# A fused transformer block and expert mixture on one core: kept sums, inverses and spreads per tile, and moves in three engines' lists

## What is computed

```python
# layer 0
h = ln(x) * (1 + sc_msa) + sh_msa
x = x + self_attn(h) * g_msa                 # 16 heads, windows of 128, rolled by 64
h = ln(x) * (1 + sc_mca) + sh_mca
q, (k, v) = h @ w_q + b_q, context @ w_kv + b_kv          # 77 context tokens
scores = q k^T / 4
top_s, top_i = top_k(scores, 16)             # of 77, for each head and token
o = softmax(top_s) @ v[top_i]
x = x + (o @ w_co + b_co) * g_mca
x = x + swiglu(ln(x) * (1 + sc_mlp) + sh_mlp) * g_mlp     # hidden 1024
# layer 1
nx = layer_norm(x) * gamma + beta
weights = softmax((nx @ Wq) (prototypes @ Wk)^T / 16)     # 77 prototypes
evidence = weights @ (prototypes @ Wv)
combined = [nx, evidence, anchor]
router_probs = softmax(combined @ router_W + router_b)    # 3 experts
h = silu(combined @ e_w1 + e_b1);  routed = sum_e router_probs_e * (h_e @ e_w2 + e_b2)
g = sigmoid(silu(combined @ gate_w1 + gate_b1) @ gate_w2 + gate_b2)
out = x + g * (routed @ out_w + out_b)
```

## Time and profile before

| | us |
|---|---|
| median of 3 runs | 1443.78 (1443.26 to 1445.39) |
| the profiled execution | 1448.53 |
| its span, first to last instruction | 1446.7 |
| PE busy | 1404.7 (97%) |
| DVE busy | 1066.6 (74%) |
| ACT busy | 818.8 (57%) |
| POOL busy | 440.5 (30%) |

### The profile page before, as it was taken

The page is one execution under the profiler, slowest core; times in us unless marked ns, Lnnn a source line. Parts: engine busy times, 40 slices in busy tenths (PEclk is TensorE's granted clock), DMA queues, the critical chain, the costliest instruction groups (busy, mean ns, idle before and its releaser), DMA issues.

```text
span 1446.7 us, 29891 instructions
## 1 busy us (share of the span) xinstructions
PE 1404.7 (97%) x9585; PEld 1177.1 (81%) x9585; DVE 1066.6 (74%) x4754; ACT 818.8 (57%) x2523; POOL 440.5 (30%) x600
## 2 busy tenths in 40 slices
PE   6999999999999999999999999999999999998997
PEld 5778788888888788888888788888888878887886
DVE  3485868788796878879697777869688786968632
ACT  2473374747556384665747466574757547474433
POOL 1314132323315232331335132232334313232302
PEclk9999999999999999999999999999999999999999
DMA  7520000010010000010010000000010000000000
GB/s 244 178 93 2 1 2 25 2 34 9 19 33 13 4 2 25 1 34 1 23 36 1 16 1 16 11 20 16 9 35 17 16 2 7 3 1 9 1 2 14
DMA packets 32760, 35.29 MB, mean 24 GB/s; under 512 B 8744, under 2 KB 27868, under 8 KB 32349
## 3 DMA queue, kind: packets, MB, share of 16 engines
q1 hardware_dynamic: 32605, 33.38, 7.6%
HBM read 28.83 MB, written 4.22 MB: 23 GB/s over the span
## 4 chain that ended last, share of the span: by engine, by line
PE 73%; DVE 21%; issue 3%; ACT 1%; POOL 1%; SPq 0%; DMA 0%; DVEq 0%; POOLq 0%; ACTq 0%
PE bank L964 16%; PE bank L1033 11%; PE bank L973 8%; PE bank L1009 7%; DVE knocked L2266 7%; PE bank L824 6%; PE bank L1016 4%; PE bank L873 4%; DVE M L2259 3%; PE bank L810 2%; PE bank L863 2%; DVE M L2254 2%; PE bank L885 2%; PE bank L781 2%; PE bank L924 2%
## 5 line engine op out<-in xcount | busy, mean ns | idle before, releaser
L964 PE MATMUL bank<-hB,Wm 128*128 128x256 f32 x1024 | 244.0, 385 | 2.5 <-ACT hB L1404 2.5
L964 PEld LDWEIGHTS bank<-hB,Wm 128*128 128x128 f32 x1024 | 191.8, 191 | 34.2 <-issue 7.0
L1009 PE MATMUL bank<-nxT,W1nx 128*128 128x256 f32 x896 | 212.6, 383 | 0.0
L1443 ACT ACTIVATE prob<-bank,rmax 128x128 f32<-128x128 f32 x512 | 180.8, 433 | 29.6 <-DVE rmax L2193 29.6
L1801 POOL TENSOR_TENSOR scores<-scores,M 128x308 f32<-128x308 f32 x128 | 94.8, 741 | 315.3 <-DVE knocked L2266 313.1
L1033 PE MATMUL bank<-W2p,gT 128*128 128x256 f32 x768 | 183.2, 381 | 3.0 <-DVE acc L2345 1.9
L1009 PEld LDWEIGHTS bank<-nxT,W1nx 128*128 128x128 f32 x896 | 166.5, 191 | 23.3 <-issue 2.8
L1033 PEld LDWEIGHTS bank<-W2p,gT 128*128 128x128 f32 x768 | 141.2, 190 | 23.8 <-issue 2.8
L1493 ACT ACTIVATE tbs<-bank,b1half 128x256 f32<-128x256 f32 x128 | 60.8, 475 | 144.6 <-PE bank L964 140.6
L1509 ACT ACTIVATE tbs<-bank,betaH 128x256 f32<-128x256 f32 x224 | 96.1, 493 | 80.2 <-PE bank L1016 79.0
L1443 ACT ACTIVATION_READ_ACCUMULATOR prob<-bank,rmax 128x1 f32 x512 | 139.7, 273 | 0.0
(11 more groups left out here) (240 smaller groups left out, 2817.6 us busy)
## 6 DMA issues: line engine op xcount, KB each, us to landing
Wm_g<-in_L_xcond_w_m_dram SPq DMA_DIRECT2D x4, 1024.0 KB, 5.4
W1ev<-in_L_xcond_e_w_dram SPq DMA_DIRECT2D x6, 512.0 KB, 7.4
x<-in_x_dram SPq DMA_DIRECT2D x16, 128.0 KB, 2.7
x<-in_x_dram SPq DMA_DIRECT2D x32, 64.0 KB, 2.3
Wm<-in_L_xcond_w_m_dram SPq DMA_DIRECT2D x1, 2048.0 KB, 9.8
out_dram<-acc SPq DMA_DIRECT2D x16, 128.0 KB, 1.7
out_dram<-acc SPq DMA_DIRECT2D x32, 64.0 KB, 2.0
batch_rows<-row_store SPq DMA_DIRECT2D x4, 384.0 KB, 3.9
```

What stands on the lines that cost most here:

```text
L964: m = pe.matmul(bank_of(name)[:, half * UT:(half + 1) * UT], Wm1[:, k, c:c + P], hB[:, k, :], start=(k == 0), stop=(k == CB - 1))
L1009: pe.matmul(bank_of(name)[:, n * UT:(n + 1) * UT], W1nx[:, k, c0 + n * P:c0 + (n + 1) * P], nxT[:, k, :], start=(n == 0 and k == 0), stop= ...
L1443: m = act.activation(prob[:, s, i, :], psum[s][:, i * P:(i + 1) * P], ACT.Exp, bias=rmax[:, t, s * HPS + i:s * HPS + i + 1], accum_out=rsu ...
```

## The change

It does six things. The kept sums are inverted tile by tile (`a_invert_kept(t, u)`), and POOL spreads them tile by tile (`a_spread_kept(t, u)`), tile 0 ahead of the shift of kept tile 1. PE waits for each tile's spread by itself, and takes the tiles in the outer loop. In PE's list the router stands ahead of the turned kept inverses, and `a_v(1)` ahead of the picks y02 and y03. In ACT's list y03's copy stands ahead of the prototype's exponential, and each `a_kept_exp` directly behind a `a_cross_exp`, so that `a_kept_exp(1)` is now ahead of `b_tanh_first("h00")`. In DVE's list the bias of the queries, the pick (1, 0) and the sum and inverse of tile 0 stand ahead of parts of the last top-k blocks.

```diff
@@ -890,11 +890,14 @@
 
             def a_turn_inverses(name, values, u):
 
-                pe.wait_ge(spread if values == "pv" else spread_x, u + 1)
                 wait_free(pe, name, u)
                 bk = bank_of(name)
-                for f in range(CB):
-                    for t in range(1 if values == "pv" and u >= 2 else TILES):
+                if values == "pv":
+                    pe.wait_ge(spread, u + 1)
+                for t in range(1 if values == "pv" and u >= 2 else TILES):
+                    if values == "xv":
+                        pe.wait_ge(spread_x, u * TILES + (t + 1))
+                    for f in range(CB):
                         v = each[values][:, t, f * (H // CB):(f + 1) * (H // CB), :].rearrange("p h d -> p (h d)")
                         m = pe.transpose(bk[:, f * UT + t * P:f * UT + (t + 1) * P], v, ident[:, :])
                 m.then_inc(full[JOB[name][0]], 1)
...
@@ -1217,11 +1220,11 @@
                 a_q(a)
                 a_v(0, a)
                 b_turn_normed(b)
+                a_v(1, a)
                 a_turn_picked(0, 2, c)
                 if r == 1:
                     pe.wait_ge(readB, batch * 5 + 5)
                 a_turn_picked(0, 3, c)
-                a_v(1, a)
                 b_proto_scores(b)
                 b_first_nx("h00", 0, b)
                 b_first_nx("h01", 2 * P, b)
...
@@ -1239,8 +1242,8 @@
                 a_turn_picked(1, 2, c)
                 a_turn_picked(1, 3, c)
                 b_first_evidence("h10", RH, b)
+                b_router(b)
                 a_turn_inverses("r2", "xv", c)
-                b_router(b)
                 a_cross_values(1, c)
                 a_scores(0, range(SLOTS), a)
                 b_first_evidence("h11", RH + 2 * P, b)
...
@@ -1654,17 +1657,17 @@
                 a_keys(a)
                 b_affine(b)
                 a_copy_picked(0, 2, c)
+                a_copy_picked(0, 3, c)
                 b_proto_exp(b)
                 a_cross_exp(1, 0, c)
-                a_copy_picked(0, 3, c)
+                a_kept_exp(0, c)
                 a_copy_values(a)
                 b_copy_weights(b)
                 a_cross_exp(1, 1, c)
-                a_kept_exp(0, c)
                 if r == 1:
                     act.wait_ge(doneB, batch + 1)
+                a_kept_exp(1, c)
                 b_tanh_first("h00", hE[:, 0], 0, 0, b)
-                a_kept_exp(1, c)
                 a_copy_picked(1, 0, c)
                 a_copy_picked(1, 2, c)
                 a_copy_picked(1, 3, c)
...
@@ -1811,16 +1814,16 @@
 
             def a_spread(values, u):
 
-                if values == "pv":
-                    pool.wait_ge(sums_inverted, u + 1)
-                    inv = rinv
-                else:
-                    pool.wait_ge(kept_inverted, u + 1)
-                    inv = kinv
+                pool.wait_ge(sums_inverted, u + 1)
                 alone(pool)
-                for t in range(1 if values == "pv" and u >= 2 else TILES):
-                    i = pool.tensor_copy(each[values][:, t], inv[:, t, :].rearrange("p (h a) -> p h a", a=1).to_broadcast([P, H, D]))
-                i.then_inc(spread if values == "pv" else spread_x, 1)
+                for t in range(1 if u >= 2 else TILES):
+                    i = pool.tensor_copy(each[values][:, t], rinv[:, t, :].rearrange("p (h a) -> p h a", a=1).to_broadcast([P, H, D]))
+                i.then_inc(spread, 1)
+
+            def a_spread_kept(t, u):
+
+                pool.wait_ge(kept_inverted, u * TILES + (t + 1))
+                pool.tensor_copy(kept[:, t], kinv[:, t, :].rearrange("p (h a) -> p h a", a=1).to_broadcast([P, H, D])).then_inc(spread_x, 1)
 
             def gate(w, n, b, done):
 
...
@@ -1953,8 +1957,9 @@
                 a_shift(1, 1, c)
                 a_shift(1, 2, c)
                 a_shift(1, 3, c)
+                a_spread_kept(0, c)
                 a_shift_kept(1, c)
-                a_spread("xv", c)
+                a_spread_kept(1, c)
                 b_mix_biases(b)
                 if r == 0:
                     gate_b(batch)
...
@@ -2230,9 +2236,9 @@
                 by_slot = ksum[:, t, :].rearrange("p (f s e) -> p s f e", f=CB, e=PAR)
                 dve.tensor_reduce(by_slot, kept[:, t].rearrange("p (s f e) k -> p s f e k", f=CB, e=PAR), AX.X, ALU.add).then_inc(kept_sum, 1)
 
-            def a_invert_kept(u):
-                dve.wait_ge(kept_sum, u * TILES + TILES)
-                dve.reciprocal(kinv[:, :, :], ksum[:, :, :]).then_inc(kept_inverted, 1)
+            def a_invert_kept(t, u):
+                dve.wait_ge(kept_sum, u * TILES + (t + 1))
+                dve.reciprocal(kinv[:, t, :], ksum[:, t, :]).then_inc(kept_inverted, 1)
 
             def a_residual(dst, src, name, u):
                 dve.wait_ge(biased[("so", "co", "mo").index(name)], u + 1)
...
@@ -2535,15 +2542,16 @@
                 b_proto_shift(b)
                 a_topk("b", 1, 1, c)
                 b_proto_norm(b)
+                a_bias_queries(a)
                 a_topk("a", 1, 3, c)
+                a_pick(1, 0, c)
                 a_topk("b", 1, 2, c)
+                a_sum_kept(0, c)
+                a_invert_kept(0, c)
                 a_topk("b", 1, 3, c)
-                a_pick(1, 0, c)
-                a_bias_queries(a)
                 a_pick(1, 1, c)
-                a_sum_kept(0, c)
                 a_sum_kept(1, c)
-                a_invert_kept(c)
+                a_invert_kept(1, c)
                 b_silu("h00", hE[:, 0], 0, b)
                 b_route_shift(b)
                 a_normalise("xv", oT2, c)
```

More of the change, by code:

```diff
@@ L1923, in prologue @@
                 a_spread("pv", 1)
-                a_spread("xv", 0)
+                a_spread_kept(0, 0)
+                a_spread_kept(1, 0)
                 rstd_of(1, EPS0, 1)
@@ L2465, in prologue @@
                 a_sum_kept(1, 0)
-                a_invert_kept(0)
+                a_invert_kept(1, 0)
                 a_normalise("pv", oT, 1)
```

3 lines of the change are left out of this document (2 added, 1 removed).

## The result

| | before | after |
|---|---|---|
| median (us) | 1444.59 | 1493.3 (1492.36 to 1494.05, 4 runs) |
| the profiled execution (us) | 1448.53 | 1493.76 |
| its span (us), mean granted clock | 1446.7, 0.990 | 1491.9, 0.969 |

The ratio after over before is 1.0333, with a 95% interval from 1.0318 to 1.0348. The median before is of four executions, one of which took 2895.49 us; of the other three it is 1443.78, the value that the forecast started from. The forecast was 1474.6, 18.7 us less than measured, and its range ended at 1493.0, 0.3 us short of the result. The sign and the wait came out as predicted; the share of the clock was put at half of what it was. The mean granted clock is 0.969 in all four executions after, so the profiled one is no odd one.

A forecast was written before the change was run, and what follows sets the result against it. TensorE (PE) was taken to bound the kernel, so a loss would be a new PE wait. 16.8 us of later y12 plus 14.0 us of clock falls gave 30.8, on 1443.8: 1474.6 us, range 1457.8 to 1493.

The forecast's parts named there:

- What bounds the kernel: PE, busy 1404.7 of 1446.7 us; each step is DVE's row to pick(1,1), then PE's row from y12.
- The exponential ahead of h00: On ACT it delays h00's drain, so PE's y12 starts late: 1.2 us per step, 16.8 us in 14.
- Sums and inverses per tile: On DVE, the first sum and inverse put 0.61 us more ahead of pick(1,1), 0.2 more in all.
- Router moved, and the edits costed at nothing: PE's 0.61 us wait for inverses goes, 14 times, 8.5 us; moved bias, second values and y03's copy cost nothing.
- D: h00 done in time, DVE's 0.61 us more cancels PE's 0.61 less: no gain or loss, 1443.8; chance 0.04.
- E: PE's 0.61 us wait goes and y12 stays in place: 8.5 us faster, 1435.3; chance 0.04.
- The last step: Cross-only last step: h00 done at 1350.97, before y12 is due at 1351.45, so no cost.
- The clock: About 2.15 us of PE idleness before y12 halves the clock in 8 of 14 steps: 14.0 us lost.
- rival C: Clock falls in nearly every step, some longer than 3.4 us: 1485 to 1493; chance 0.12.
- The base: Forecast starts from the median of three runs, 1443.8 us; the profiled execution lies 4.7 us above it.

The follow-up runs named there:

- e5: The changed kernel with 9 unused identity products on PE filling the wait between y10 and y12 in the 14 steps; 1462.5 us.
- e1: The changed kernel with only the exponential of kept tile 1 put back behind h00's tanh group on ACT; 1450.12 us.
- e2: The kernel before with only the exponential of kept tile 1 moved ahead of h00's tanh group on ACT; 1444.17 us.
- e6: The changed kernel with DVE's order of bias, picks and sums, and POOL's shift ahead of the spread, as before; sums still per tile; 1436.37 us.
- e3: The changed kernel with DVE's order of bias, picks and sums as before, sums still per tile, POOL's order left as changed; 1539.39 us.
- e8: The changed kernel with only the bias of the queries put back behind the last top-k block on DVE; 1452.75 us.
- e7: As e6, with the bias of the queries behind the second pick on DVE, and y10 turned and copied after y12 and y13; 1444.16 us.

## Why the prediction was right in kind and too small

**What bounds the kernel.** Held. The wait for POOL went, and a wait before y12 took its place, released by h00's last instruction.

**The exponential ahead of h00.** Held to a tenth. With the shift of 2.69 us between the two profiles, the prediction's times are: last top-k block 260.70, POOL's shift 261.56, h00 drained 264.13, y12 264.19, cross values 266.64. The rows have 260.71, 261.53, 264.05, 264.19 and 266.67. The growth of a step without a fall was to be 1.2 us (14 x 1.2 = 16.8); it was 1.24 in the three such steps, and 17.5 over 14 in e5. e1 and e2 show that both halves are needed.

**Sums and inverses per tile.** Slightly off: DVE's pick(1,1) came 262.26 - 2.69 - 258.79 = 0.78 us later, not 0.61. The block itself came on time, so the 0.17 arose between its start and the pick. The rows place it. Pick(1,1) now stands directly behind the block whose last replacement it waits for, and starts 0.33 us after that replacement's start (261.93, 262.26). Before, pick(1,0) stood there, which needs nothing of this block, and started 0.14 after it (257.16, 257.30); in e6 it is 0.14 again, and in e1 0.34. In after it is hidden behind ACT's wait; in e1 it counts: 0.78 later on DVE less the 0.61 at the inverses is 0.17, measured 0.19 a step.

**Router moved, and the edits costed at nothing.** Held: the wait of 0.61 is gone, and e6 shows its worth undisturbed, 0.58 a step. One small thing was missed: PE now reaches the prototype's weights (L997) earlier than DVE has them (DVE's norm starts at 252.90 before and at 255.59 - 2.69 = 252.90 after), the 3.3 us of waits named above. The rivals D (no change) and E (8.5 us faster) were not wrong as places, but as states of this kernel: they need h00 drained in time, and that is what e1 and e6 establish. E gave 1435.3; e6 gave 1436.4.

**The last step.** Held: 14 waits, not 15, and all growth lies in the 14 steps.

**The clock: the term that was mis-sized.** I took 8 falls at 1.75 us, 14.0 us. There were 11, worth 27.9. Two factors. The number: I let the single row of 2.19 us of idleness stand for about half of the steps, and at 2.16 to 2.48 it was 11 of 14. The length, which weighs more: I took 3.4 us at half clock from the earlier trace rows for each, and 7 of the 11 lasted 6.8. A fall of 3.4 us cost 1.5 rather than 1.75. (The price of the row itself was sound: its 32 matmuls take 8.86 us with the fall, and 7.17 in e6, where none came, 1.69 less.) Eleven falls of 1.5 us would have been 16.5; the seven long ones add the rest, 1.6 us each. The prediction had this in rival C ("some lasting longer than 3.4 us, as the stretch of small matmuls behind the wait might"), whose end was the nearest to the time, but gave it 0.12. What spoke for it was in view: behind the wait of the earlier trace rows stood 32 matmuls of 128x256, and behind the new one stand transposes, 3-column products and 32-row products. That this is what made seven falls last longer is argued, not shown: the three kinds of step (0, 3.4, 6.8 us) have the same instructions behind the wait, and no run changed what stands there.

The Trainium skill (TensorE: Matmul & The Clock Gate, section "HAM oscillation — how this bites in real kernels"), which the prediction cites, describes waits of about 3 to 5 us, once in each iteration, with the clock down behind every one. The traces agree for waits of that length: it fell behind the wait of 3.54 us in the last cross step in all 12 kernels profiled, and in all 14 steps of e3 with 3.63 us or more. That is no forecast for the 2.2 us here, which are shorter, and behind which it fell in 11 of 14.

**The base.** The sum was 30.8 us; profile against profile it was 45.2. That is 14.4 us of the 18.7 missed, nearly all of it the clock (27.9 against 14.0). The other 4.3 are the base: before's profiled execution lay 4.7 us above the 1443.8 that the forecast started from, and after's only 0.5 above its median. The spread of before goes with the granted clock: the 14 executions beside e8 have a mean of 0.990 in those at 1448 us and of 0.992 in those at 1443 to 1444. Why it differs there stays open.

## What to carry to other kernels

Moving an instruction to the front of a list is safe only if what it waits for is also early, in the same version of the kernel: ask of each moved instruction what releases it there, and which engine waits for the one now behind it. Here one move was harmless without the other (0.2 us) and cost 42.8 us with it; the link between them, a bank that passes from h00 to y12, appeared in no wait of the profile of before. A gain can also hide a loss: DVE's order cost 10.9 us, and the 8.3 us won by the rest of the change left 2.6 of it to be seen. When an order is changed on one engine, walk the chain through every other list that feeds or follows it (e3: one POOL instruction left in its place cost 100 us against e6), and price a wait on TensorE of about 2 us with the clock as well as with its own length: the clock's share was here larger than the wait's.

## What the hardware showed that I had not expected

**Half clock costs more than the wait, and useless work is cheaper than idleness.** The wait before y12 lengthens the steps by 17.5 us, the falls behind it by 27.9. Nine products in each step that nothing reads made the kernel 31 us faster. Idleness at this place against falls, over all kernels:

| idle us at the place | falls |
|---|---|
| 0.15 to 0.5 (e5, after the filler), 0.5 to 0.6 (e7), 0.7 to 0.95 and 0.5 (e8), 1.1 to 1.3 (e1) | none in 14 steps each |
| 2.16 to 2.48 (after) | 11 of 14 |
| 3.63 to 3.70, in the last cross step 2.92 (e3) | 15 of 15 |

**The same wait falls or not.** Steps with the same instructions and 2.16 us (step 2, no fall) or 2.17 us (step 3, 6.8 us at 0.50) of idleness behave differently. The waits behind the 14 steps show the same. They are alike in all 12 kernels profiled: the clock fell behind the one of 3.54 or 3.55 us in 12 of 12, behind the one of 2.19 us (`hB`) in 7 of 12, and behind one of 1.03 us in 3 of 12 (after, e6 and e7). In e6 it was the longer one that passed, and the shorter one that was followed by 0.50:

```profile
1367.20 7.17 PE L967 MATMUL bank<-hB,Wm 128*128 128x256 f32 x32 [2.19 <-ACT hB L1407]
...
1407.46 3.54 PE L1036 MATMUL bank<-W2p,gT 128*128 128x256 f32 x8 [1.03 <-ACT gT L1519]
```

The eight matmuls of the second row took 1.99 us in before, behind the same 1.03 us of idleness. So the table above is no threshold, and the lack of falls in e1 is what happened in its 14 steps, not a safe length. What decides is not in these rows; it stays open.

**A POOL shift beside a pick.** POOL's shift of slot (1,3) took 1.20 us in after, beside DVE's pick(1,0); in before such shifts took 0.70 to 0.91, with a median of 0.71. It was not on the path. No run isolates it.
